# A linear-attention and FFN layer on eight cores: the bf16 copy of x goes from ScalarE to VectorE, the weight ring gets a sixth slot, and the hand-placed early weight loads go

## The chip, the cores and the metric

The kernel runs on all 8 cores of one Trainium2 chip. Each core runs the same program on its own tokens and nothing is exchanged between cores. The metric is the device time of the slowest core, in microseconds (us). PE is TensorE, ACT is ScalarE, DVE is VectorE, POOL is GpSimd and SP is SyncE; PEld is the weight load of TensorE.

## The reference

```python
xn = layernorm(x)                       # x: (4, 4096, 1024) f32, over the last axis, no scale or bias

qkv = xn @ Wqkv + bqkv                  # attention part
q, k, v = split(qkv, 3)
q = q / norm(q);  k = k / norm(k)
kv = sum(k * v, axis=tokens)            # one vector of 1024 for each batch
attn = (q * kv) @ Wout + bout

h = silu(xn @ w1.T * s1) * (xn @ w2.T * s2)      # FFN part, 1024 -> 4096
h = gelu(h @ h1.T * t1)                          # 4096 -> 4096
h = gelu(h @ h2.T * t2)                          # 4096 -> 4096
ffn = h @ w3.T * s3                              # 4096 -> 1024

out = x + attn + ffn
```

## The kernel before

**Tiles.** Two cores share one batch of 4096 tokens. A core writes the output of its own 2048 tokens, but the sum over tokens `kv` needs k and v of all 4096, so it computes those for the other half too. Everything is kept feature-major: features on the 128 partitions, 1024 tokens (`TT`) in the free dimension. The 4096 tokens are four groups g = 0 to 3 of 1024 tokens; 0 and 1 are the core's own. A group of x is 8 chunks (`DC`) of 128 features by 1024 tokens, 512 KB each in f32. The normalised chunks of a group lie in bf16 in one of three regions of the large buffer `Gb` (`REGION`, `xn_sl`).

**Statistics of a group** (`plan_stats`, line 201). For each of the 8 chunks: SP loads the chunk into one of two slots `xs` (`dma_x`, line 181); ACT copies it to bf16 into its region (line 211) and frees the slot; ACT squares the copy into one of two slots `sq` (line 222); PE multiplies a matrix of ones by the copy into PSUM `PA` (the sum) and, two chunks behind, by the square into `PB` (`qmm`, line 237). That is four 128x512 matmuls a chunk. Then DVE and ACT form mean and inverse deviation (lines 250 to 264), and DVE rewrites the 8 chunks in place as normalised values, two operations each (`emit_xn`, lines 273 and 276).

**Weights.** All weights come as units of 128x2048, 1 MB of f32 in HBM, cast to bf16 (512 KB) by a DMA that POOL issues (`dma_w`, line 189) into a ring of five slots `wr`. A load waits until the unit that lay in the slot has been used by PE, and POOL issues strictly in program order.

**Order of the work.** The program is written out by hand, and each engine follows it in order. `Sched.op` adds a wait on the engine's own last operation to every ACT and DVE instruction. First block:

1. statistics of group 0, then loads of the four k units. The first of these loads waits for nothing; the other three have a gate (line 408): they wait for PE's sum over chunks 1, 3 and 5 of group 0;
2. k projection of group 0 (`plan_proj` with `k_evac`), whose results ACT moves out of PSUM and squares; the loads of the four v units, with a gate on the sum over the last chunk of group 0 (line 463); the norm of k (ACT Ln and Exp, lines 319 and 323);
3. statistics of group 1, v projection of group 0, `plan_kv` (DVE: k times v times norm, summed over tokens);
4. k projection of group 1, its norm, statistics of group 2, q projection of group 0, v projection of group 1, `plan_kv` again.

Then all engines meet at the end of the block. The second block begins with the statistics of group 3 and the first FFN layer (w1, w2), goes on with k and v of groups 2 and 3, the layers h1, h2, and the last layer with Wout and w3, and repeats the FFN for the second 1024 tokens.

Two orders matter here. On ACT, the copies of group 1 stand behind the 16 evictions and squares of the k projection and behind Ln and Exp; so do those of group 2. On POOL, a load that waits holds up all loads behind it.

```python
            st["pre_k"] = [dma_w(wqkv[4, :, :])] + [
                dma_w(wqkv[4 + i, :, :], gate=ck0[2 * i - 1][0]) for i in (1, 2, 3)]
```

Of the kernel before, what the change touches and what calls it, by code (L numbers as in the profile page):

```python
# [7 lines left out]
BF16 = mybir.dt.bfloat16  # L8
AF = mybir.ActivationFunctionType
# [4 lines left out]
TT = 1024  # L14
# [5 lines left out]
REGION = {0: 0, 1: 1, 2: 2, 3: 1, 4: 0, 5: 2}  # L20
# [86 lines left out]
def build_program(stop=None):  # L107
    nc = bass.Bass("TRN2", target_bir_lowering=False)

    x_hbm = nc.dram_tensor("x_fm", [D, T], F32, kind="ExternalInput").ap()  # L110
    wqkv = nc.dram_tensor("wqkv_t", [12, 128, 2048], F32, kind="ExternalInput").ap()
# [12 lines left out]
    with ExitStack() as _ctx:  # L124
# [11 lines left out]
        tmp_f = en(nc.sbuf_tensor("tmp_f", [128, TT], F32))  # L136
        xs0 = en(nc.sbuf_tensor("xs0", [128, TT], F32))
        xs1 = en(nc.sbuf_tensor("xs1", [128, TT], F32))
        xb0 = en(nc.sbuf_tensor("xb0", [128, TT], BF16))
        xb1 = en(nc.sbuf_tensor("xb1", [128, TT], BF16))  # L140
        sq0 = en(nc.sbuf_tensor("sq0", [128, TT], BF16))
        sq1 = en(nc.sbuf_tensor("sq1", [128, TT], BF16))
        sil0 = en(nc.sbuf_tensor("sil0", [128, TT], BF16))
# [8 lines left out]
        PB = en(nc.psum_tensor("PB", [128, TT], F32))  # L152
        PC = en(nc.psum_tensor("PC", [128, TT], F32))
        PD = en(nc.psum_tensor("PD", [128, TT], F32))
        semnames = ["s_xa", "s_xb", "s_wa", "s_wb", "s_wc", "s_wd", "s_we",
                    "s_oa", "s_ob", "s_ini", "s_pe", "s_dv", "s_ac", "s_po",
                    "s_ba", "s_bb"]
        sem_h = {n: en(nc.semaphore(n)) for n in semnames}
# [1 line left out]
        dma_sems = [n for n in semnames if n not in ("s_pe", "s_dv", "s_ac")]  # L160
        S = Sched(nc, sem_h, dma_sems)
        xs_ring = Ring([xs0, xs1], ["s_xa", "s_xb"])
        xb_ring = Ring([xb0, xb1], ["s_ba", "s_bb"])
        sq_ring = Ring([sq0, sq1])
        sil_ring = Ring([sil0])
        os_ring = Ring([os0, os1], ["s_oa", "s_ob"])
        w_ring = Ring([wr0, wr1, wr2, wr3, wr4], ["s_wa", "s_wb", "s_wc", "s_wd", "s_we"])
        PS = {"PA": PA, "PB": PB, "PC": PC, "PD": PD}
        psum_free = {k: None for k in PS}
        war = {0: None, 1: None, 2: None}  # L170
# [4 lines left out]
        def xn_sl(g, kc, hh=None):  # L175
            base = REGION[g] * DC * TT + kc * TT
            if hh is None:
                return Gb[:, base: base + TT]
            return Gb[:, base + hh * 512: base + (hh + 1) * 512]
# [9 lines left out]
        def dma_w(unit_ap, gate=None):  # L189
            j, slot, ftok = w_ring.next()  # L190
            tok = S.op("gpsimd", lambda e, o=slot, i=unit_ap: e.dma_start(out=o[:, :], in_=i),  # L191
                       waits=[ftok, gate], inc=w_ring.semn[j])
            return j, slot, tok
# [7 lines left out]
        def plan_stats(g, psS="PA", psQ="PB", defer_xn=False, via_region=True):  # L201
            t0 = T0MAP[g]
            pend = []
            last_q = [None]
            chunk_toks = {}
            for c in range(DC):
                if len(pend) >= 2:
                    pend.pop(0)()
                jx, xslot, tx = dma_x(c, t0)
                if via_region:  # L210
                    tb = S.op("scalar", lambda e, g_=g, c_=c, i=xslot: e.activation(  # L211
                        xn_sl(g_, c_), i[:, :], AF.Identity),
                        waits=[tx, war[REGION[g]]], inc="s_ac")
                    sq_src = xn_sl(g, c)
                else:
                    jb, bslot, fb = xb_ring.next()
                    tb = S.op("vector", lambda e, o=bslot, i=xslot: e.tensor_copy(o[:, :], i[:, :]),
                              waits=[tx, fb], inc="s_dv")
                    sq_src = bslot[:, :]
                xs_ring.set_free(jx, tb)  # L220
                jq, qslot, fq = sq_ring.next()
                tq = S.op("scalar", lambda e, o=qslot, i=sq_src: e.activation(o[:, :], i, AF.Square),
                          waits=[tb, fq], inc="s_ac")
                tok_s = None
                for hh in range(2):
                    rhs = xn_sl(g, c, hh) if via_region else bslot[:, hh * 512:(hh + 1) * 512]
                    tok_s = mm(psS, hh, ones_sb[:, :], rhs,
                               start=(c == 0), stop=(c == DC - 1),
                               waits=[tb, psum_free[psS]],
                               inc="s_pe" if hh == 1 else None)  # L230
                if via_region:
                    chunk_toks[c] = [tok_s, tq]
                    st["chunk_toks_%d" % g] = chunk_toks
                else:
                    xb_ring.set_free(jb, [tok_s, tq])

                def qmm(c_=c, jq_=jq, qslot_=qslot, tq_=tq):
                    tok_c = None
                    for hh in range(2):
                        tok_c = mm(psQ, hh, ones_sb[:, :], qslot_[:, hh * 512:(hh + 1) * 512],  # L240
                                   start=(c_ == 0), stop=(c_ == DC - 1),
                                   waits=[tq_, psum_free[psQ]],
                                   inc="s_pe" if hh == 1 else None)
                    sq_ring.set_free(jq_, tok_c)
                    last_q[0] = tok_c
                pend.append(qmm)
            while pend:
                pend.pop(0)()
            t_stats = last_q[0]
            t1 = S.op("vector", lambda e, p=psS: e.tensor_scalar(  # L250
                tmp_f[:, :], PS[p][:, :], float(1.0 / D), None, ALU.mult),
                waits=[t_stats, st["act_tmp_u"]], inc="s_dv")
            t2 = S.op("scalar", lambda e: e.activation(u_b[:, :], tmp_f[:, :], AF.Square),
                      waits=[t1], inc="s_ac")
            t3 = S.op("vector", lambda e, p=psQ: e.scalar_tensor_tensor(  # L255
                rstd_b[:, :], PS[p][:, :], float(1.0 / D), u_b[:, :], ALU.mult, ALU.subtract),
                waits=[t2], inc="s_dv")
            psum_free[psS] = t1
            psum_free[psQ] = t3
            t4 = S.op("scalar", lambda e: e.activation(rstd_b[:, :], rstd_b[:, :], AF.Ln, bias=f32(EPS)),  # L260
                      waits=[t3], inc="s_ac")
            t5 = S.op("scalar", lambda e: e.activation(rstd_b[:, :], rstd_b[:, :], AF.Exp, scale=f32(-0.5)),
                      waits=[t4], inc="s_ac")
            t6 = S.op("vector", lambda e: e.tensor_mul(u_b[:, :], tmp_f[:, :], rstd_b[:, :]),
                      waits=[t5], inc="s_dv")
            st["act_tmp_u"] = t2
            st["stats_t5t6"] = (t5, t6)
            xn_toks = []
            xn_toks_g[g] = xn_toks

            def emit_xn(c):
                if via_region:
                    ta = S.op("vector", lambda e, g_=g, c_=c: e.tensor_mul(
                        tmp_f[:, :], xn_sl(g_, c_), rstd_b[:, :]),
                        waits=[t5], inc="s_dv")
                    tb2 = S.op("vector", lambda e, g_=g, c_=c: e.tensor_tensor(  # L276
                        xn_sl(g_, c_), tmp_f[:, :], u_b[:, :], ALU.subtract),
                        waits=[ta, t6, chunk_toks[c]], inc="s_dv")
                else:
                    jx, xslot, tx = dma_x(c, t0)  # L280
                    ta = S.op("vector", lambda e, i=xslot: e.tensor_mul(tmp_f[:, :], i[:, :], rstd_b[:, :]),
                              waits=[tx, t5], inc="s_dv")
                    tb2 = S.op("vector", lambda e, g_=g, c_=c: e.tensor_tensor(
                        xn_sl(g_, c_), tmp_f[:, :], u_b[:, :], ALU.subtract),
                        waits=[ta, t6, war[REGION[g]]], inc="s_dv")
                    xs_ring.set_free(jx, ta)
                xn_toks.append(tb2)

            if defer_xn:
                return emit_xn  # L290
            for c in range(DC):
                emit_xn(c)
# [89 lines left out]
        with (  # L382
# [6 lines left out]
            def plan_kv(kbuf, vbuf, t_rk, kev, vev, rbuf):  # L389
# [13 lines left out]
                    st["kv_dve_par0"] = st["kv_done"]  # L403

            plan_stats(0, "PA", "PB")
            ck0 = st["chunk_toks_0"]
            st["pre_k"] = [dma_w(wqkv[4, :, :])] + [
                dma_w(wqkv[4 + i, :, :], gate=ck0[2 * i - 1][0]) for i in (1, 2, 3)]
            xn_toks_g[4] = xn_toks_g[0]
            for t in range(NT1):  # L410
                kbuf = qkvt if t % 2 == 0 else kB2
# [40 lines left out]
                def v_evac(oc, ps, t_mm, _vb=vbuf, _vev=vev):  # L452
# [6 lines left out]

                plan_proj([(wqkv[4 + i, :, :], [2 * i, 2 * i + 1]) for i in range(4)],  # L460
                          t, k_evac, pre=st.get("pre_k"))
                if t == 0:
                    st["pre_v"] = [dma_w(wqkv[8 + i, :, :],
                                         gate=st["chunk_toks_0"][7][0])
                                   for i in range(4)]
                while pend_n:
                    pend_n.pop(0)()
                if t == 0:
# [6 lines left out]
                if t == NT1 - 1:  # L475
                    plan_qproj(4)
                plan_proj([(wqkv[8 + i, :, :], [2 * i, 2 * i + 1]) for i in range(4)],
                          t, v_evac, pre=st.pop("pre_v", None))
                war[t % 3] = S.pe_tok()
                st["pre_k"] = ([dma_w(wqkv[4 + i, :, :], ) for i in range(4)]  # L480
                               if t + 1 < NT1 else None)
# [361 lines left out]
```

How the kernel before makes its waits and increments, by code:

```python
            def body(eng):  # L69
                for _, fn, waits, tok in items:
                    for wt in waits:
                        sname, val = wt[0], wt[1]
                        key = (ename, sname)
                        if self.done.get(key, 0) >= val:
                            continue
                        eng.wait_ge(self.sems[sname], val)
                        self.done[key] = val
                    if fn is not None:
                        inst = fn(eng)
                        if tok is not None:
                            inst.then_inc(self.sems[tok[0]],
                                          16 if tok[0] in self.DMA_SEMS else 1)
```

## Time and profile before

| | us |
|---|---|
| median of two runs | 3010.55 (3009.04 and 3012.05) |
| the profiled execution | 3009.54 |
| its span on the slowest core (core 5), first to last instruction | 3008.0 |
| spans of the eight cores | 2983.2 to 3008.0 |
| PE busy on core 5 | 2859.7 (95%), 13024 matmuls |
| ACT, DVE busy on core 5 | 487.0 (16%), 347.2 (12%) |
| mean granted clock of TensorE, eight cores | 0.973 to 0.982 |

The span is what the trace shows of the profiled execution; 1.5 us of its time lie around it. All rows below are of core 5, and their times count from the start of its span.

### The profile page before, as it was taken

What the parts mean: (1) busy time and instruction counts of PE and PEld (TensorE: products, weight loads), DVE (VectorE), ACT (ScalarE), POOL (GpSimd) and SP (SyncE); (2) the same over time, 40 slices, a digit from 0 to 9 for tenths busy, and PEclk for the clock granted to TensorE, in tenths of its full rate; (3) what the DMA queues carried; (4) which work ended last, traced back from release to release, by engine and by line L of the source; (5) the groups of instructions that cost most, each with busy time, mean ns of one, the idle gap of its engine ahead of it and who ended that gap; (6) DMA issues with size and microseconds to landing.
All of it is one profiled execution on the core that took longest, in us unless ns stands there. A gap on an engine that the chain in (4) does not pass through costs nothing.

```text
span 3008.0 us, 30367 instructions; the slowest of 8 cores (2983.2 to 3008.0 us)
## 1 busy us (share of the span) xinstructions
PE 2859.7 (95%) x13024; PEld 1276.6 (42%) x13024; DVE 347.2 (12%) x397; ACT 487.0 (16%) x484; POOL 219.9 (7%) x420
## 2 busy tenths in 40 slices
PE   3887899999999999999997899999999999999998
PEld 0332344444444444444443344444444444444443
DVE  3244111451000000000002121100000000000011
ACT  3564211541000000000000131110000000000000
POOL 0000000110000000000000000000000000000000
PEclk7888999999999999999998999999999999999999
DMA  4444344874444444444446644444444444444454
GB/s 107 113 90 91 67 75 78 156 129 82 76 76 77 77 78 77 77 75 75 76 78 139 132 70 79 72 79 76 77 77 77 77 78 77 76 75 75 77 113 104
DMA packets 71412, 260.04 MB, mean 86 GB/s; under 512 B 8176, under 2 KB 8304, under 8 KB 71280
## 3 DMA queue, kind: packets, MB, share of 16 engines
q0 software_dynamic: 59904, 218.13, 43.2%
q1 hardware_dynamic: 11376, 39.97, 4.3%
q8 instruction: 105, 1.72, 0.2%
q14 instruction: 27, 0.22, 0.0%
HBM read 466.74 MB, written 9.44 MB: 158 GB/s over the span
## 4 chain that ended last, share of the span: by engine, by line
PE 85%; DMA 3%; DVE 1%; ACT 1%; issue 0%; SPq 0%; DVEq 0%; ACTq 0%
PE PD L198 24%; PE PC L198 24%; PE PA L198 19%; PE PB L198 19%; DMA xs<-x_fm 2%; DMA out_fm<-os 1%; DVE os L761 1%; DVE os L755 0%; ACT os L727 0%; ACT Gb L211 0%; SPq L765 0%; ACT Gb L590 0%; DVE Ab L540 0%; ACT L617 0%; DVE Gb L697 0%
## 5 line engine op out<-in xcount | busy, mean ns | idle before, releaser
L198 PE MATMUL PC<-Gb,wr 128*128 128x512 bf16 x2080 | 476.9, 382 | 22.5 <-DVE Gb L276 22.5
L198 PE MATMUL PD<-Gb,wr 128*128 128x512 bf16 x2080 | 474.0, 380 | 0.0
L198 PE MATMUL PB<-Gb,wr 128*128 128x512 bf16 x1728 | 392.1, 380 | 4.2 <-DVE rstd_b L255 4.2
L198 PE MATMUL PD<-Ab,wr 128*128 128x512 bf16 x1536 | 352.8, 383 | 31.3 <-ACT os L727 31.3
L198 PE MATMUL PA<-Gb,wr 128*128 128x512 bf16 x1536 | 347.2, 379 | 0.0
L198 PE MATMUL PC<-Ab,wr 128*128 128x512 bf16 x1536 | 347.2, 379 | 0.0
L198 PEld LDWEIGHTS PC<-Gb,wr 128*128 128x128 bf16 x2080 | 203.7, 98 | 274.4 <-issue 32.7
L198 PEld LDWEIGHTS PD<-Gb,wr 128*128 128x128 bf16 x2080 | 204.4, 98 | 247.2 <-issue 3.8
L198 PEld LDWEIGHTS PB<-Gb,wr 128*128 128x128 bf16 x1728 | 169.2, 98 | 210.0 <-issue 7.0
L191 POOL DMA_DIRECT2D wr<-h_t x256 | 135.1, 528 | 1616.6 <-PE PB L198 797.2
L198 PEld LDWEIGHTS PD<-Ab,wr 128*128 128x128 bf16 x1536 | 151.3, 99 | 218.1 <-issue 41.7
L198 PE MATMUL PA<-Ab,wr 128*128 128x512 bf16 x1024 | 231.4, 379 | 2.9 <-DVE Ab L540 1.7
L198 PE MATMUL PB<-Ab,wr 128*128 128x512 bf16 x1024 | 231.5, 379 | 0.0
L198 PEld LDWEIGHTS PC<-Ab,wr 128*128 128x128 bf16 x1536 | 150.3, 98 | 181.2
L198 PEld LDWEIGHTS PA<-Gb,wr 128*128 128x128 bf16 x1536 | 150.1, 98 | 181.4
L198 PEld LDWEIGHTS PA<-Ab,wr 128*128 128x128 bf16 x1024 | 99.9, 98 | 124.3 <-issue 3.8
L198 PEld LDWEIGHTS PB<-Ab,wr 128*128 128x128 bf16 x1024 | 100.1, 98 | 120.9
L755 DVE SCALAR_TENSOR_TENSOR os<-PC,cst,os 128x1024 f32<-128x1024 f32 x8 | 10.3, 1284 | 1079.3 <-PE PC L198 1079.3
L697 DVE TENSOR_TENSOR Gb<-tmp_f,u_b 128x1024 bf16<-128x1024 f32 x8 | 9.8, 1225 | 857.9 <-PE PD L198 857.2
L191 POOL DMA_DIRECT2D wr<-w_t x96 | 50.7, 528 | 697.5 <-PE PD L198 565.3
L198 PE MATMUL PA<-Gb,ones_sb 128*128 128x512 bf16 x64 | 31.5, 594 | 68.3 <-ACT Gb L211 68.3
L668 ACT ACTIVATE Ab<-PA,cst 128x1024 bf16<-128x1024 f32 x16 | 17.8, 1114 | 404.9 <-PE PB L198 404.9
(88 smaller groups left out, 1001.5 us busy)
## 6 DMA issues: line engine op xcount, KB each, us to landing
wr<-h_t POOLq DMA_DIRECT2D x256, 512.0 KB, 5.6
wr<-w_t POOLq DMA_DIRECT2D x96, 512.0 KB, 5.2
xs<-x_fm SPq DMA_DIRECT2D x56, 512.0 KB, 5.3
wr<-wqkv_t POOLq DMA_DIRECT2D x56, 512.0 KB, 6.0
out_fm<-os SPq DMA_DIRECT2D x16, 512.0 KB, 3.2
wr<-wout_t POOLq DMA_DIRECT2D x8, 512.0 KB, 7.4
ustats_scratch<-u_b SPq DMA_DIRECT2D x1, 512.0 KB, 3.7
ustats_scratch<-rstd_b SPq DMA_DIRECT2D x1, 512.0 KB, 8.0
```

Of the source, the lines that this page charges most:

```text
L191: tok = S.op("gpsimd", lambda e, o=slot, i=unit_ap: e.dma_start(out=o[:, :], in_=i), waits=[ftok, gate], inc=w_ring.semn[j])
L198: e.matmul(p[:, h * 512:(h + 1) * 512], l, r, start=a, stop=b),
L668: t_g = S.op("scalar", lambda e, o=oc, p=ps: e.activation(dst[:, o * TT:(o + 1) * TT], PS[p][:, :], AF.Gelu, scale=s_cst[:, s_col0 + o:s_c ...
L697: tb2 = S.op("vector", lambda e, c_=c: e.tensor_tensor(xn_sl(5, c_), tmp_f[:, :], u_b[:, :], ALU.subtract), waits=[ta, t_lr, war[REGION[5] ...
L755: t2o = S.op("vector", lambda e, p=ps, o=oslot, c=oc: e.scalar_tensor_tensor(o[:, :], PS[p][:, :], cst2[:, 32 + c:33 + c], o[:, :], ALU.mu ...
L761: t3o = S.op("vector", lambda e, o=oslot, x_=xslot: e.tensor_add(o[:, :], o[:, :], x_[:, :]), waits=[t2o, tx], inc="s_dv")
```

## The change

It does three things. The bf16 copy of each x chunk in `plan_stats` becomes a DVE `tensor_copy` (shown as CAST) in place of an ACT activation; the square stays on ACT. The buffers `xb0` and `xb1`, whose path was never taken, go, and in their place a sixth weight slot `wr5` joins the ring. The lists `pre_k` (first use) and `pre_v`, with their gates, go: the loads are now issued where the projections ask for them, with no wait but that for a free slot.

```diff
-        xb0 = en(nc.sbuf_tensor("xb0", [128, TT], BF16))
-        xb1 = en(nc.sbuf_tensor("xb1", [128, TT], BF16))
+        wr5 = en(nc.sbuf_tensor("wr5", [128, 2048], BF16))
...
-        w_ring = Ring([wr0, wr1, wr2, wr3, wr4], ["s_wa", "s_wb", "s_wc", "s_wd", "s_we"])
+        w_ring = Ring([wr0, wr1, wr2, wr3, wr4, wr5],
+                      ["s_wa", "s_wb", "s_wc", "s_wd", "s_we", "s_wf"])
...
                 if via_region:
-                    tb = S.op("scalar", lambda e, g_=g, c_=c, i=xslot: e.activation(
-                        xn_sl(g_, c_), i[:, :], AF.Identity),
-                        waits=[tx, war[REGION[g]]], inc="s_ac")
+                    tb = S.op("vector", lambda e, g_=g, c_=c, i=xslot: e.tensor_copy(
+                        xn_sl(g_, c_), i[:, :]),
+                        waits=[tx, war[REGION[g]]], inc="s_dv")
...
             plan_stats(0, "PA", "PB")
-            ck0 = st["chunk_toks_0"]
-            st["pre_k"] = [dma_w(wqkv[4, :, :])] + [
-                dma_w(wqkv[4 + i, :, :], gate=ck0[2 * i - 1][0]) for i in (1, 2, 3)]
...
-                if t == 0:
-                    st["pre_v"] = [dma_w(wqkv[8 + i, :, :],
-                                         gate=st["chunk_toks_0"][7][0])
-                                   for i in range(4)]
...
                 plan_proj([(wqkv[8 + i, :, :], [2 * i, 2 * i + 1]) for i in range(4)],
-                          t, v_evac, pre=st.pop("pre_v", None))
+                          t, v_evac)
```

The places where instructions move:

POOL at the start of the program, before: the first load waits only for the constants (`s_ini`), the others for PE (`s_pe`).

```order
5 L191 DMA wr0<-wqkv_t 128x2048 [waits s_ini]
6 L191 DMA wr1<-wqkv_t 128x2048 [waits s_pe]
7 L191 DMA wr2<-wqkv_t 128x2048 [waits s_pe]
8 L191 DMA wr3<-wqkv_t 128x2048 [waits s_pe]
9 L191 DMA wr4<-wqkv_t 128x2048 [waits s_pe]
10 L191 DMA wr0<-wqkv_t 128x2048 [waits s_pe]
```

The same place now:

```order
5 L190 DMA wr0<-wqkv_t 128x2048 [waits s_ini]
6 L190 DMA wr1<-wqkv_t 128x2048
7 L190 DMA wr2<-wqkv_t 128x2048
8 L190 DMA wr3<-wqkv_t 128x2048
9 L190 DMA wr4<-wqkv_t 128x2048
10 L190 DMA wr5<-wqkv_t 128x2048
11 L190 DMA wr0<-wqkv_t 128x2048 [waits s_pe]
```

Six loads now stand one behind the other with no wait between them; the first wait on PE comes with the seventh.

ACT before, from the end of the k projection of group 0 (eviction into `qkvt`, its square), over Ln and Exp (lines 319, 323), into the statistics of group 1:

```order
34 L430 ACTIVATE qkvt<-PD,cst 128x1024
35 L435 ACTIVATE sq<-qkvt 128x1024
36 L319 ACTIVATE rstdn_b<-PA 128x1024
37 L323 ACTIVATE rstdn_b<-rstdn_b 128x1024
38 L211 ACTIVATE Gb<-xs 128x1024
39 L222 ACTIVATE sq<-Gb 128x1024
```

ACT now, the same place and on to the end of the statistics:

```order
19 L420 ACTIVATE qkvt<-PD,cst 128x1024
20 L425 ACTIVATE sq<-qkvt 128x1024
21 L312 ACTIVATE rstdn_b<-PA 128x1024
22 L316 ACTIVATE rstdn_b<-rstdn_b 128x1024
23 L218 ACTIVATE sq<-Gb 128x1024 x8
24 L246 ACTIVATE u_b<-tmp_f 128x1024
```

Of the pair copy and square, eight times over, only the eight squares are left behind Exp.

DVE now, from the last normalised chunk of group 0 on (with its waits; `s_xa` and `s_xb` are the loads into the two `xs` slots, `s_dv` is DVE's own):

```order
27 L266 TENSOR_TENSOR tmp_f<-Gb,rstd_b 128x1024 [waits s_dv]
28 L269 TENSOR_TENSOR Gb<-tmp_f,u_b 128x1024 [waits s_dv]
29 L210 CAST Gb<-xs 128x1024 [waits s_xa,s_dv]
30 L210 CAST Gb<-xs 128x1024 [waits s_xb,s_dv]
31 L210 CAST Gb<-xs 128x1024 [waits s_xa,s_dv]
```

The copies of group 1 wait for their loads and for DVE's own work, and no longer stand behind ACT's evictions, nor do they wait for PE.

## Rows read from the trace of the kernel before

**Rows 1.** Waits of PE: for whom, us in total, times, longest; last row included.

```profile
PE PA L198 <- ACT Gb L211: 68.3, 32, 11.3
PE PD L198 <- ACT os L727: 31.3, 6, 10.7
PE PC L198 <- DVE Gb L276: 22.5, 8, 10.9
...
PE PA L198 <- ACT sq L603: 0.4, 1, 0.4
```

**Rows 2.** Stretch, length, busy of PE, PEld, DVE, ACT, POOL, PEclk, DMA, GB/s.

```profile
0.00:315.00 315.00, 215.48 (x816) 81.54 (x816) 113.71 (x124) 156.89 (x146) 13.54 (x29) 0.80 0.44 99
```

**Rows 3.** Timeline of group 1's statistics: start, us, instruction, [idle before, releaser].

```profile
96.75 1.03 PE L198 MATMUL PA<-sq,ones_sb 128*128 128x512 bf16 x4
...
101.39 1.06 ACT L323 ACTIVATE rstdn_b<-rstdn_b 128x1024 f32<-128x1024 f32 x1
102.54 1.06 ACT L211 ACTIVATE Gb<-xs 128x1024 bf16<-128x1024 f32 x1
...
107.36 1.06 ACT L211 ACTIVATE Gb<-xs 128x1024 bf16<-128x1024 f32 x1 [0.33 <-DMA xs<-x_fm]
...
121.58 1.06 ACT L211 ACTIVATE Gb<-xs 128x1024 bf16<-128x1024 f32 x1 [0.44 <-DMA xs<-x_fm]
...
123.59 1.91 PE L198 MATMUL PB<-sq,ones_sb 128*128 128x512 bf16 x4
125.29 4.76 PE L198 MATMUL PC<-Gb,wr 128*128 128x512 bf16 x16
```

**Rows 4.** Timeline around group 2's statistics: end of DVE's `plan_kv`, Exp, q projection.

```profile
177.82 0.16 DVE L398 TENSOR_TENSOR kv_acc<-kv_acc,kvp 128x1 f32<-128x1 f32 x1
...
188.48 1.06 ACT L323 ACTIVATE rstdn_c<-rstdn_c 128x1024 f32<-128x1024 f32 x1
...
211.93 4.11 PE L198 MATMUL PC<-Gb,wr 128*128 128x512 bf16 x16
```

**Rows 5.** Timeline: DVE's last normalised chunk of group 0.

```profile
65.74 1.23 DVE L276 TENSOR_TENSOR Gb<-tmp_f,u_b 128x1024 bf16<-128x1024 f32 x1
```

**Rows 6.** Loads into `xs` from 185 to 212 us, no weight load beside them.

```profile
DMA to landing us min/median/max: 3.5/4.2/4.3
```

**Rows 7.** Timeline of group 0's statistics: first two weight loads, last copy, its end.

```profile
5.36 0.66 POOL L191 DMA_DIRECT2D wr<-wqkv_t  x1 [4.66 <-DMA ones_sb<-ones_bf]
...
15.02 0.53 POOL L191 DMA_DIRECT2D wr<-wqkv_t  x1 [9.00 <-PE PA L198]
...
33.65 1.06 ACT L211 ACTIVATE Gb<-xs 128x1024 bf16<-128x1024 f32 x1 [1.12 <-DMA xs<-x_fm]
...
37.82 1.23 DVE L250 TENSOR_SCALAR tmp_f<-PA 128x1024 f32<-128x1024 f32 x1 [36.61 <-PE PB L198]
```

**Rows 8.** DMA queues, 0 to 45 us: packets, MB, share of 16 engines.

```profile
q1 hardware_dynamic: 1872, 5.36, 39.2%
q0 software_dynamic: 720, 2.62, 35.4%
```

**Rows 9.** Busy time by stretch, the first 40 us, columns as in rows 2.

```profile
0.00:20.00 20.00, 4.74 (x10) 1.01 (x10) 0.07 (x1) 8.37 (x8) 1.39 (x6) 1.00 0.70 156
20.00:40.00 20.00, 9.46 (x22) 2.34 (x22) 1.23 (x1) 10.62 (x11) 1.58 (x3) 0.80 0.87 222
```

**Rows 10.** Loads into `xs` from 276 to 312 us, with three weight loads beside them.

```profile
DMA to landing us min/median/max: 3.5/4.4/11.5
```

**Rows 11.** Timeline, second block: weight loads, group 3's third copy, first FFN matmuls.

```profile
278.26 1.06 POOL L191 DMA_DIRECT2D wr<-w_t  x2 [24.70 <-POOLq L85]
...
279.60 0.53 POOL L191 DMA_DIRECT2D wr<-w_t  x1 [0.28 <-issue]
...
294.49 1.06 ACT L211 ACTIVATE Gb<-xs 128x1024 bf16<-128x1024 f32 x1 [8.27 <-DMA xs<-x_fm]
...
315.69 5.10 PE L198 MATMUL PB<-Gb,wr 128*128 128x512 bf16 x16 [4.15 <-DVE rstd_b L255]
```

More of the change, by code:

```diff
@@ L154, in build_program @@
         PD = en(nc.psum_tensor("PD", [128, TT], F32))
-        semnames = ["s_xa", "s_xb", "s_wa", "s_wb", "s_wc", "s_wd", "s_we",
+        semnames = ["s_xa", "s_xb", "s_wa", "s_wb", "s_wc", "s_wd", "s_we", "s_wf",
                     "s_oa", "s_ob", "s_ini", "s_pe", "s_dv", "s_ac", "s_po",
@@ L162, in build_program @@
         xs_ring = Ring([xs0, xs1], ["s_xa", "s_xb"])
-        xb_ring = Ring([xb0, xb1], ["s_ba", "s_bb"])
         sq_ring = Ring([sq0, sq1])
@@ L210, in plan_stats @@
                 if via_region:
-                    tb = S.op("scalar", lambda e, g_=g, c_=c, i=xslot: e.activation(
-                        xn_sl(g_, c_), i[:, :], AF.Identity),
-                        waits=[tx, war[REGION[g]]], inc="s_ac")
+                    tb = S.op("vector", lambda e, g_=g, c_=c, i=xslot: e.tensor_copy(
+                        xn_sl(g_, c_), i[:, :]),
+                        waits=[tx, war[REGION[g]]], inc="s_dv")
                     sq_src = xn_sl(g, c)
                 else:
[L216 to L219, printed above, removed]
+                    raise NotImplementedError("xb path removed")
                 xs_ring.set_free(jx, tb)
@@ L230, in plan_stats @@
                                inc="s_pe" if hh == 1 else None)
[L231 to L235, printed above, removed]
+                chunk_toks[c] = [tok_s, tq]
+                st["chunk_toks_%d" % g] = chunk_toks
                 def qmm(c_=c, jq_=jq, qslot_=qslot, tq_=tq):
```

## The prediction

> **What bounds the kernel now.** I read the waits of PE first, because PE is busy for 95% of the span: only what PE waits for, and the clock it runs at, can be won. Its longest item is the 68.3 us, in 32 waits, for ACT's bf16 copy of an x chunk; then 31.3 us for an output slot in the last layer and 22.5 us for DVE's normalised chunks at the start [rows 1]. The list ends at 0.4 us, and nobody in it waits for a weight load. All 32 waits for copies lie in the first 315 us, where PE is busy for 215 us and its mean granted clock is 0.80 [rows 2]. The rest of the program is PE at its pace.
>
> So I went through the timeline of the four statistics phases. For group 1, ACT ends Exp at 101.39 + 1.06 = 102.45, begins the first copy at 102.54, and PE starts the next projection at 125.29: 22.8 us for eight chunks [rows 3]. A chunk costs there (121.58 - 107.36) / 5 = 2.84 us: load, copy and square in turn, through two slots. Group 2 shows the same: Exp ends at 189.54, the projection starts at 211.93, 22.4 us [rows 4].
>
> **Part 1: the copies on DVE, group 1.** Behind Exp, ACT keeps eight squares. Its operations follow one another every 102.54 - 101.39 = 1.15 us [rows 3], so the squares take 9.2 us, and the last one's matmuls about 1 us more: 10.2. PE has four matmuls a chunk: 1.03 us for four at full clock, 1.91 at the low clock [rows 3]. At full clock ACT sets the pace. If PE stayed at the low clock, it would set it: 1.15 + 8 x 1.91 = 16.4. I take 11.5, near the first, because PE then has work all the time and three slow chunks, 3 x (1.91 - 1.03) = 2.6, half hidden, would add 1.3 (an estimate). Gain 22.8 - 11.5 = 11.3, between 6.4 and 12.6.
>
> This needs the copies to be done in time. DVE's last normalised chunk of group 0 ends at 65.74 + 1.23 = 67.0 [rows 5], and at 2.84 a chunk the eight copies of group 1 end by 89.7, 12.7 us before Exp ends. That time of DVE lies beside the k projection. The trace shows no cast on DVE. Its bounds are DVE's smallest operation, 0.16 [rows 4], and its usual 128x1024 operation, 1.23 [rows 5]; ACT's copy took 1.06 [rows 3]. I take 1.23, the nearest in shape. What is queued behind the casts on DVE is the mean of group 1, which waits for PE's last square anyway.
>
> The Trainium skill (VectorE: DVE Perf Modes, the perf-mode tier table) says that a tensor_copy of fp32 in SBUF runs at twice the rate of a two-tensor operation; from its figures I estimate 0.69 us for this cast. No row here shows it. By that price only group 3 changes, by 2 us, and the sum below would be 2993.
>
> **Part 2: group 2.** The casts stand behind `plan_kv` of group 0 on DVE, which ends at 177.98, 11.6 us before Exp [rows 4]. Two chunks lie ready, six follow at 2.84: 177.98 + 2 x 1.23 + 6 x 2.84 = 197.5, 7.9 us after Exp. The eighth square could begin 8.1 us after Exp, so loads and squares arrive together. The pace agrees with the landing of 4.2 us alone [rows 6]: (4.2 + 1.23) / 2 = 2.7. I take 11.9 in place of 22.4: gain 10.5. Bounds: no chunk late, gain 12; PE at the low clock, gain 6.
>
> **Part 3: the weight loads at the start.** Here the change costs. Before, the second load is held until PE releases it at 15.02, and so on; the last copy of group 0 begins at 33.65 [rows 7]. Now six loads go out at once. The queues' shares give the price in time of the 16 engines: x loads 0.392 x 45 / 10 = 1.76 us each (the queue also carried the small constants), weight loads 0.354 x 45 / 5 = 3.19 us each [rows 8]. Until 33.65, eight x loads and four weight loads are 14.1 + 12.8 = 26.9 us in the 28.6 us from about 5 on: 94% busy. With six it is 33.2 us, at 94% 35.3, and the last chunk lands near 40.4: 7 us later. Everything behind it (mean, deviation, the normalised chunks for which PE waits) moves with it, as PE has nothing else to do there. The lower bound is 0: the DMA share over the first 40 us is 0.70 and 0.87 [rows 9], which leaves 8.6 us free, and the two further loads are 6.4. The upper bound: all six first, 5 + 19.1 + 3.5 for the two chunks in front = 27.6, the third chunk at 29.4, five more at 2.84, 43.6: 10 us. I stay with 7, since in the second block a chunk of x issued behind three weight loads took 11.5 us to land, in place of 4.2 [rows 6, 10]: x does not come first.
>
> The Trainium skill (DMA: Bandwidth & Descriptors, Queues, rings and completion order) says that each DMA engine takes turns between its queues packet by packet. With equal packets x would have 1.76 / (1.76 + 3.19) = 0.36 of the time, and a chunk would take some 4.9 us; the 11.5 us of rows 10 say that it was served worse than that. By the rule the last chunk would land near 38.3 and the sum would be 2993.
>
> What the early loads bring is nothing: PE never waited for one. POOL has nothing behind them but later loads.
>
> **Part 4: group 3.** It opens the second block, and its region is free only then, so nothing moves ahead. With six slots four weight loads go out there instead of three (two and one) [rows 11], 3.19 us more in front of chunks 2 to 7: a loss of 0 to 3.2. From the third copy at 294.49 to the first FFN matmul at 315.69 are 21.2 us [rows 11]. With casts beside the squares: two slot rounds of 1.23 + 4.2, the last pair of casts 2.5, a square 1.1, its matmuls 1, and the same 4.2 of mean and deviation give 19.7 to 20, a gain of 1.4; were the casts shorter, up to 3.4. I count 0, between 3 lost and 3.4 gained.
>
> **Part 5: the sixth slot elsewhere.** Each load is still released by the end of a unit, one load per unit; only the unit it brings is one further on. As PE waits for none of them, this is 0. If this cover were missing, a late load would cost PE up to its 3.19 us.
>
> **Sum.** - 11.3 - 10.5 + 7 + 0 = - 14.8. Against the profiled execution's 3009.54: 2994.7, say 2995. The median of the runs is 1.0 above that execution, inside their spread of 3, so I leave it there. Which core ends last is decided in the last layer, by the waits for output slots, which differ between cores; I allow some 3 us for that.
>
> **Rivals.**
> - The early loads cost nothing and the casts are short: gains 12.6 and 12, the start 0, group 3 + 3.4: 28 us, 2981.5. For it: the free DMA share of rows 9. Against: rows 10.
> - The PE clock stays low in the statistics, so PE paces them: 6.4 + 6 - 7 = 5.4 us gained, 3004. For it: the four matmuls at 123.59 took 1.91 [rows 3]. Against: there PE waited between chunks, and now it would not.
> - Slower: the bursts starve x. If a chunk behind six loads takes twice the 11.5 us of rows 10, the third chunk of group 0 lands near 33, five more at 2.84 give 47: 13.4 us late. The fourth load of the second block costs a third of 11.5, 3.8, less 1.4. With the low gains of 12.4: 13.4 + 2.4 - 12.4 = 3.4 us slower, 3013. It decides from the point where group 0's last cast begins after about 46 us. For it: all eight cores send their bursts at the same time. Against: the DMA engines would have to stand idle, and rows 9 show them busy.
>
> **Chances.** Forecast 0.50; cheap start 0.20; low clock 0.20; starved x 0.08; 0.02 for anything else. The range from 2979 to 3011 takes in the first three with the scatter of the cores and part of the fourth. All of them lie within 2% (60 us, about what a measurement of this kernel can tell from no change): faster by over 2% 0.02, within 0.96, slower by over 2% 0.02.
>
> **What would show it.** Right: PE's waits for the copies fall from 68.3 us to under 35, and some return as waits for squares; from the end of the k norm's Exp to the next projection 11 to 12 us twice; the first mean of group 0 (37.82 before) near 45; group 1's casts done before Exp. Wrong: group 0's mean before 40 or after 50; 16 us from Exp to the projections; casts that wait for loads while PE stands; any wait of PE for a weight load.

## The result, and the profile after

The changed kernel took 2999.8 us (median of 12 runs, lowest 2992.08), the kernel before beside it 3014.51 us (11 runs, lowest 3007.84). The ratio, which leaves disturbed runs out, is 0.9942 with a 95% interval of 0.9926 to 0.9959: 17.5 us faster by 3010, between 12 and 22, or 0.6%. The forecast of 2995 against 3009.54 is a ratio of 0.9952, 14.8 us.

The first place to look is the list of PE's waits. The profiled execution of the changed kernel took 3000.44 us; its slowest core is core 3, with a span of 2998.9 (columns as in [rows 1]).

```profile
PE PA L197 <- DVE Gb L210: 63.1, 16, 11.8
PE PD L197 <- ACT os L713: 29.0, 6, 8.1
PE PC L197 <- DVE Gb L269: 22.5, 8, 10.6
...
PE PB L197 <- ACT sq L218: 2.7, 4, 1.3
```

The wait for the copy is now for DVE, in 16 places instead of 32, but its sum has hardly fallen: 63.1 against 68.3 [rows 1]. By stage, on these two cores, it went from 23.4 to 31.7 in the first 45 us, from 20.5 to 3.5 in groups 1 and 2, and from 24.5 to 27.9 at group 3. So the gain cannot be read from the sum, and the phases must be taken one by one. A mark that every run has is the start of the mean of a group (the DVE operation out of `PA` that follows the last square, line 250 before, 243 after). Read from the timelines and averaged over the eight cores:

| start of the mean, us | group 0 | group 1 | group 2 | group 3 | 0 to 1 | 1 to 2 | 2 to 3 |
|---|---|---|---|---|---|---|---|
| before | 39.7 | 126.5 | 212.9 | 312.5 | 86.8 | 86.5 | 99.6 |
| after | 46.7 | 121.6 | 198.3 | 300.0 | 74.8 | 76.7 | 101.7 |

Group 0 is 7.0 us later, the next two steps are 11.9 and 9.8 us shorter, the last is 2.2 us longer. At the last mark 12.5 us are won.

**Start, timeline of core 3.** The answer to [rows 7]:

```profile
5.23 3.31 POOL L190 DMA_DIRECT2D wr<-wqkv_t  x6 [4.53 <-DMA ones_sb<-ones_bf]
...
10.48 0.69 DVE L210 CAST Gb<-xs 128x1024 bf16<-128x1024 f32 x1 [9.28 <-DMA xs<-x_fm]
...
22.97 0.69 DVE L210 CAST Gb<-xs 128x1024 bf16<-128x1024 f32 x1 [9.72 <-DMA xs<-x_fm]
...
42.89 0.69 DVE L210 CAST Gb<-xs 128x1024 bf16<-128x1024 f32 x1 [2.10 <-DMA xs<-x_fm]
...
45.77 1.23 DVE L243 TENSOR_SCALAR tmp_f<-PA 128x1024 f32<-128x1024 f32 x1 [2.18 <-PE PB L197]
```

Six loads are issued in 3.31 us, and DVE then stands 9.72 us before the third chunk. The landing times of the x loads in the first 45 us, against a median of 4.2 alone [rows 6]:

```profile
DMA to landing us min/median/max: 3.6/6.9/14.1
```

What the 16 DMA engines did meanwhile, same core: queues (as in [rows 8]) and the loads issued, from 11.5 to 14.9 us:

```profile
q0 software_dynamic: 141, 0.53, 101.2%
q1 hardware_dynamic: 3, 0.00, 0.0%
...
xs<-x_fm SPq DMA_DIRECT2D x2, 512.0 KB, 12.8
```

Then from 15 to 35 us:

```profile
q0 software_dynamic: 609, 2.21, 69.1%
q1 hardware_dynamic: 476, 1.75, 32.7%
```

The busy time of 15 to 35 and of 35 to 45 us, columns as in [rows 2]:

```profile
15.00:35.00 20.00, 4.00 (x9) 0.88 (x8) 1.58 (x3) 2.11 (x2) 0.00 (x0) 1.00 1.02 198
35.00:45.00 10.00, 6.50 (x17) 1.65 (x18) 2.58 (x4) 4.22 (x4) 0.00 (x0) 1.00 0.71 200
```

While the third and fourth chunk wait, the weight queue (q0) at first has the engines to itself; afterwards x (q1) has about a third of their time. (A packet counts whole where it starts, so a share can come out slightly over 100%.)

**Group 1, same core.** The answer to [rows 3]:

```profile
98.26 0.69 DVE L210 CAST Gb<-xs 128x1024 bf16<-128x1024 f32 x1 [3.60 <-DMA xs<-x_fm]
...
109.20 1.06 ACT L316 ACTIVATE rstdn_b<-rstdn_b 128x1024 f32<-128x1024 f32 x1
...
110.35 2.20 ACT L218 ACTIVATE sq<-Gb 128x1024 bf16<-128x1024 bf16 x2
...
111.55 1.01 PE L197 MATMUL PB<-sq,ones_sb 128*128 128x512 bf16 x2 [1.27 <-ACT sq L218]
...
112.71 1.06 ACT L218 ACTIVATE sq<-Gb 128x1024 bf16<-128x1024 bf16 x1 [0.16 <-PE PB L197]
...
113.21 1.06 PE L197 MATMUL PB<-sq,ones_sb 128*128 128x512 bf16 x2
...
114.42 5.65 ACT L218 ACTIVATE sq<-Gb 128x1024 bf16<-128x1024 bf16 x5 [0.65 <-PE PB L197]
...
115.66 0.59 PE L197 MATMUL PB<-sq,ones_sb 128*128 128x512 bf16 x2
...
120.64 3.62 PE L197 MATMUL PC<-Gb,wr 128*128 128x512 bf16 x16
```

The last cast is over at 98.95, 11 us before Exp ends at 110.26. From there to the projection it takes 10.4 us where it took 22.8. The first two pairs of matmuls for squares still run at the low clock (1.01 and 1.06 us a pair), and ACT waits 0.16 and 0.65 us for them. From the third pair on they run at the full one (0.59 in the row at 115.66, the fourth pair), and ACT's last five squares go through in 5.65 us, 1.13 each: from there ACT sets the pace. The projection's 16 matmuls now begin at full clock, 3.62 us against 4.76.

**Group 2, same core.** The answer to [rows 4]:

```profile
173.38 0.16 DVE L391 TENSOR_TENSOR kv_acc<-kv_acc,kvp 128x1 f32<-128x1 f32 x1
173.65 1.49 DVE L210 CAST Gb<-xs 128x1024 bf16<-128x1024 f32 x2
...
182.69 1.06 ACT L316 ACTIVATE rstdn_c<-rstdn_c 128x1024 f32<-128x1024 f32 x1
...
187.22 0.69 DVE L210 CAST Gb<-xs 128x1024 bf16<-128x1024 f32 x1 [5.44 <-DMA xs<-x_fm]
...
194.28 0.69 DVE L210 CAST Gb<-xs 128x1024 bf16<-128x1024 f32 x1 [1.89 <-DMA xs<-x_fm]
...
197.63 4.79 PE L197 MATMUL PC<-Gb,wr 128*128 128x512 bf16 x16
```

Here the loads are late. DVE waits 5.44 us for the fifth chunk, the eighth is cast 10.5 us after Exp ends, and Exp to projection takes 13.9 us. Two weight loads, issued at 170.98 and 178.75, go out beside these chunks; x lands there in 5.5 us at the median and 6.5 at most, against 4.2 with no weight load beside it [rows 6].

**Group 3, same core.** The answer to [rows 11]:

```profile
264.63 2.12 POOL L190 DMA_DIRECT2D wr<-w_t  x4 [34.80 <-POOLq L85]
...
283.30 0.69 DVE L210 CAST Gb<-xs 128x1024 bf16<-128x1024 f32 x1 [10.60 <-DMA xs<-x_fm]
...
298.14 0.69 DVE L210 CAST Gb<-xs 128x1024 bf16<-128x1024 f32 x1 [2.71 <-DMA xs<-x_fm]
...
305.85 5.26 PE L197 MATMUL PB<-Gb,wr 128*128 128x512 bf16 x16 [4.15 <-DVE rstd_b L248]
```

Four loads go out instead of three. The third cast comes 18.7 us after the first of them is issued; before, the third copy came 16.2 us after. From it to the FFN it is 22.6 us, against 21.2: all casts wait for x.

### The profile page after: what moved, and what is told of

It reads as the page before. It is cut to its first block, busy times and chain, and to the rows that moved or that the text cites. A ratio compares the mean times of both kernels' runs of the same rounds, so it can differ in the third digit from the quotient of the medians.

```text
span 2998.9 us, 30424 instructions; the slowest of 8 cores (2966.1 to 2998.9 us)
## 1 busy us (share of the span) xinstructions
PE 2852.4 (95%) x13024; PEld 1276.3 (43%) x13024; DVE 369.2 (12%) x429; ACT 453.2 (15%) x452; POOL 220.0 (7%) x420
## 4 chain that ended last, share of the span: by engine, by line
PE 85%; DMA 4%; DVE 1%; ACT 1%; issue 0%; SPq 0%; DVEq 0%; ACTq 0%
PE PD L197 24%; PE PC L197 24%; PE PB L197 19%; PE PA L197 19%; DMA xs<-x_fm 2%; DMA out_fm<-os 1%; DVE os L747 1%; DVE os L741 0%; ACT os L713 0%; DVE Gb L210 0%; SPq L751 0%; ACT Gb L576 0%; DVE Ab L526 0%; ACT L603 0%; DVEq L76 0%
## 5 line engine op out<-in xcount | busy, mean ns | idle before, releaser
L197 PEld LDWEIGHTS PA<-Ab,wr 128*128 128x128 bf16 x1024 | 99.9, 98 | 124.3 <-issue 3.8
L197 PE MATMUL PA<-Gb,ones_sb 128*128 128x512 bf16 x64 | 26.7, 517 | 66.1 <-DVE Gb L210 63.1
L654 ACT ACTIVATE Ab<-PC,cst 128x1024 bf16<-128x1024 f32 x16 | 17.8, 1114 | 405.2 <-PE PD L197 405.2
```

The lines of the kernel that those rows point to most:

```text
L197: e.matmul(p[:, h * 512:(h + 1) * 512], l, r, start=a, stop=b),
L654: t_g = S.op("scalar", lambda e, o=oc, p=ps: e.activation(dst[:, o * TT:(o + 1) * TT], PS[p][:, :], AF.Gelu, scale=s_cst[:, s_col0 + o:s_c ...
```

## The experiments

Theory: the terms are separate. The moved copies win some 11 and 10 us in groups 1 and 2, the early loads cost some 7 at the start, the sixth slot costs a little in the second block and wins nothing. Rivals: the start is late because the copies moved; a part of the gain comes from weights that lie there earlier; the early loads pay back later what they cost. The marks below are averages over the eight cores as in the table above; the ratios are to the kernel before, run beside each kernel on the same chip.

**1. The copies alone.** The kernel before, with only this edit:

```diff
-                    tb = S.op("scalar", lambda e, g_=g, c_=c, i=xslot: e.activation(
-                        xn_sl(g_, c_), i[:, :], AF.Identity),
-                        waits=[tx, war[REGION[g]]], inc="s_ac")
+                    tb = S.op("vector", lambda e, g_=g, c_=c, i=xslot: e.tensor_copy(
+                        xn_sl(g_, c_), i[:, :]),
+                        waits=[tx, war[REGION[g]]], inc="s_dv")
```

Expected:

> The kernel before with the copies of x on VectorE and nothing else: five weight slots, the gates on the early weight loads kept. Measure: start of the mean (TENSOR_SCALAR out of PA) of groups 0 to 3, averaged over the eight cores; before 39.7, 126.5, 212.9 and 312.5 us, after the change 46.8, 121.6, 198.3 and 300.0. Theory (the terms are separate, and the start's 7 us come from six weight loads ahead of x): group 0 at 39 to 40; group 0 to 1 74 to 76 us and group 1 to 2 76 to 78, as after the change; group 2 to 3 98 to 101. The mean of group 3 falls to 288 to 294, so 18 to 24 us faster than before, ratio 0.992 to 0.994. Rival (the start is late because the copies moved): group 0 at 45 to 48, the rest as after the change, group 3 near 300. Rival (a part of the 12 and 10 us won in groups 1 and 2 comes from weights that were loaded earlier or from the sixth slot): the steps from group to group stay above 79 us.

Measured: means at 37.2, 112.8, 190.0 and 289.9; steps 75.5, 77.3, 99.9; ratio 0.9903 (0.9871 to 0.9935). The slowest core's timeline, first and last mean:

```profile
35.60 1.23 DVE L250 TENSOR_SCALAR tmp_f<-PA 128x1024 f32<-128x1024 f32 x1 [2.30 <-PE PB L198]
...
287.71 1.22 DVE L250 TENSOR_SCALAR tmp_f<-PA 128x1024 f32<-128x1024 f32 x1 [3.04 <-PE PB L198]
```

Nearly the whole gain of groups 1 and 2 is there without early loads and without the sixth slot (11.2 of 11.9 and 9.2 of 9.8), so the second rival falls. The start is not late but 2.5 us early, below the range that the theory gave: the copies do not hurt it, they help. Group 3 gains nothing. The ratio lies below the expected 0.992 to 0.994, which its interval takes in.

**2. The early loads alone.** The kernel before without `pre_k` and `pre_v`, five slots, copies on ACT:

```diff
-            st["pre_k"] = [dma_w(wqkv[4, :, :])] + [
-                dma_w(wqkv[4 + i, :, :], gate=ck0[2 * i - 1][0]) for i in (1, 2, 3)]
...
-                          t, v_evac, pre=st.pop("pre_v", None))
+                          t, v_evac)
```

Expected:

> The kernel before without the gates and lists of early loads, copies still on ScalarE, five slots: five weight loads go out at once at the start. Theory: group 0's mean at 43 to 47 (before 39.7), as one load fewer than after the change stands ahead of x; the steps from group to group as before (86.8, 86.5, 99.6 us, each within 1.5); so 4 to 7 us slower than before, ratio 1.001 to 1.003. Rival (the loads are harmless and the moved copies make the start late): group 0 at 39 to 40.5, ratio 1.000.

Measured: means at 45.7, 132.5, 219.5 and 320.8; steps 86.8, 87.0, 101.2; ratio 1.0031 (1.0004 to 1.0058). Timeline of its slowest core: five loads, the third copy, the mean.

```profile
5.28 2.78 POOL L191 DMA_DIRECT2D wr<-wqkv_t  x5 [4.58 <-DMA ones_sb<-ones_bf]
...
24.21 1.06 ACT L211 ACTIVATE Gb<-xs 128x1024 bf16<-128x1024 f32 x1 [8.10 <-DMA xs<-x_fm]
...
46.79 1.23 DVE L250 TENSOR_SCALAR tmp_f<-PA 128x1024 f32<-128x1024 f32 x1 [45.59 <-PE PB L198]
```

ACT stands 8.10 us before its third copy, as DVE does after the change, although the copies have not moved. The start is 6.0 us late, and none of it comes back in the next two steps; the step from group 2 to 3 is 1.7 us longer, a little over the 1.5 allowed, though three loads go out there as before. The first rival falls.

**3. The sixth slot alone.** In the place of the unused buffers:

```diff
-        xb0 = en(nc.sbuf_tensor("xb0", [128, TT], BF16))
-        xb1 = en(nc.sbuf_tensor("xb1", [128, TT], BF16))
+        wr5 = en(nc.sbuf_tensor("wr5", [128, 2048], BF16))
```

Expected:

> The kernel before with a sixth weight slot in the place of the unused xb buffers, gates and copies as before. Theory: the sixth slot buys nothing, and one more load stands ahead of x in the second block: means of groups 0 to 2 as before within 1 us, group 3 1 to 3.5 us later (step from group 2 to 3 101 to 103 in place of 99.6), ratio 1.000 to 1.002. Rival (a deeper ring takes loads out of the way of the last layer's stores, or hides some): ratio below 0.998 with a step from group 2 to 3 as before.

Measured: means at 40.6, 128.0, 215.2 and 316.8; steps 87.4, 87.2, 101.6; ratio 1.0009 (0.9987 to 1.0031). The step from group 2 to 3 is 2.0 us longer, as foretold, but run 2 shows 1.7 in this step without a fourth load, so the 2.0 is hardly clear of the scatter; groups 0 to 2 drifted by 0.9 to 2.2 us, a little more than expected. No gain shows anywhere.

**4. All but the early loads.** The changed kernel with the two lists and their gates put back:

```diff
+            st["pre_k"] = [dma_w(wqkv[4, :, :])] + [
+                dma_w(wqkv[4 + i, :, :], gate=ck0[2 * i - 1][0]) for i in (1, 2, 3)]
...
-                          t, v_evac)
+                          t, v_evac, pre=st.pop("pre_v", None))
```

Expected:

> The changed kernel with the gates on the early loads put back: copies on VectorE, six slots. Theory: as the run with the copies alone, but with the fourth load in the second block: group 0 at 39 to 40, steps 74 to 76 and 76 to 78, step from group 2 to 3 1 to 3 us longer than in that run; group 3's mean at 291 to 296, 6 to 9 us ahead of the changed kernel; ratio to the kernel before 0.992 to 0.995. Rival (the ungated loads pay back later what they cost at the start): no gain over the changed kernel, group 3's mean at 299 to 301.

Measured: means at 37.6, 113.2, 191.1 and 292.6; steps 75.6, 77.9, 101.5; ratio 0.9908 (0.9877 to 0.9939). It is 7.4 us ahead of the changed kernel at the last mark, and 9.1 us at the first. So the early loads cost 9.1 us where the casts are on DVE, and 1.7 of it comes back on the way. Run 2 lost 6.0 with five loads; the 3.1 more are about the 3.19 us of one load, the sixth, for which the sixth slot makes room, but this was not tried apart. The third rival falls, but for those 1.7. Group 0 came 1.4 us earlier and the ratio lower than expected, as in run 1. The total time does not tell runs 1 and 4 from the changed kernel, as the intervals overlap: what the early loads cost rests on the marks.

**5. Fewer loads beside x at the start.** Run 1, with the three gates on the last chunk's sum:

```diff
-                dma_w(wqkv[4 + i, :, :], gate=ck0[2 * i - 1][0]) for i in (1, 2, 3)]
+                dma_w(wqkv[4 + i, :, :], gate=ck0[7][0]) for i in (1, 2, 3)]
```

Expected:

> The run with the copies alone, with the gates of the three later k loads moved to PE's sum over the last chunk of group 0: one weight load instead of four stands beside the eight x loads at the start. Theory (each load beside x costs about its 3.2 us of the DMA engines, down to the pace of the two slots, (4.2 + 0.69) / 2 = 2.45 us a chunk): group 0's mean at 29 to 33 us (copies alone 37.2, before 39.7), the steps as in the run with the copies alone (75.5, 77.3, 99.9), as the k units still land before PE asks for them; 4 to 8 us faster than that run, ratio to the kernel before 0.987 to 0.991. Rival (the start is bound by the two slots and the landing, not by the loads): group 0 at 36 to 38. Rival (the loads are then late): PE waits for a weight load, step from group 0 to 1 above 77.

Measured: means at 33.5, 109.0, 187.0 and 287.1; steps 75.5, 78.0, 100.1; ratio 0.9901 (0.9877 to 0.9924). Timeline of the slowest core: the four held loads, the mean.

```profile
31.99 2.11 POOL L191 DMA_DIRECT2D wr<-wqkv_t  x4 [26.27 <-PE PA L198]
33.32 1.23 DVE L250 TENSOR_SCALAR tmp_f<-PA 128x1024 f32<-128x1024 f32 x1 [3.04 <-PE PB L198]
```

The loads leave only when the last chunk of group 0 is summed, and no wait of PE for a weight load is in the list. The start wins 3.7 us more, just short of the least that was expected: with few loads beside x, the two slots would set the pace, which run 7 tries. The total hardly differs from run 1's, where 4 to 8 us were expected; the 2.8 us by which the last mark is ahead are too few for it to show.

**6. No weight loads beside group 3.** Run 5, and in the second block:

```diff
-                        jw1, w1slot, tw1 = dma_w(w1[gc, :, :])
-                        jw2, w2slot, tw2 = dma_w(w2[gc, :, :])
+                        g3 = st["chunk_toks_3"][7][0] if (t == 0 and gc in (1, 2)) else None
+                        jw1, w1slot, tw1 = dma_w(w1[gc, :, :], gate=g3)
+                        jw2, w2slot, tw2 = dma_w(w2[gc, :, :], gate=g3)
```

Expected:

> As the run with late gates, and in the second block the weight loads of w1 and w2 units 1 and 2 wait for PE's sum over the last chunk of group 3, so none stands beside group 3's x loads. Theory: a chunk there then lands in about 4.2 us instead of 11, so the step from group 2 to 3 falls from 99.9 to 90 to 94; nothing of it is given back later, as the first FFN units take 13.8 us from the loads already there; ratio 0.983 to 0.988. Rival (the late loads make PE wait in the first FFN layer): the step falls as said, but the mean span of the cores does not follow it.

Measured: means at 33.5, 108.8, 185.6 and 276.7; steps 75.3, 76.8, 91.1; ratio 0.989 (0.9869 to 0.9911). The landing times of group 3's x loads on its slowest core, against 3.5/4.4/11.5 [rows 10]:

```profile
DMA to landing us min/median/max: 3.6/3.9/5.9
```

Without weight loads beside them no chunk takes 11 us. The last step is 9.0 us shorter than in run 5. The only wait of PE for a weight load on that core is one of 0.9 us. The total moved less than the marks, just outside the expected ratio; the mean span of the eight cores in the profiled executions fell from 2967.4 to 2963.2, 4.2 of the 10.4 us. So the sign of the rival came (the mean span does not follow), but not its cause. The rest went in the last layer: at ACT's first evictions into `os` run 6 is still 10.2 us ahead of run 5, behind the last layer of the first 1024 tokens 4.4, at ACT's last eviction 4.5 (averages over the eight cores). PE's waits for an output slot are 20.2 us there on average, 16.4 in run 5; they differ by more than that from core to core, and whether this is more than scatter was not tried.

**7. A third x slot.** Run 6, with the bytes of the unused buffers given to x:

```diff
+        xs2 = en(nc.sbuf_tensor("xs2", [128, TT], F32))
...
-        xs_ring = Ring([xs0, xs1], ["s_xa", "s_xb"])
+        xs_ring = Ring([xs0, xs1, xs2], ["s_xa", "s_xb", "s_xc"])
```

Expected:

> As the run before it, with a third slot for x chunks in the bytes that the change gave to the sixth weight slot. Theory: where no weights stand beside x, the pace falls from 2.45 us a chunk towards the engines' 1.76: group 0's mean at 25 to 28, step from group 0 to 1 as before (75.5: the copies were in time), step from group 1 to 2 75 to 76 (the last chunks of group 2 no longer late), step from group 2 to 3 86 to 91; ratio 0.979 to 0.986. Rival (HBM, not the slots, sets the pace, as all cores load at once): group 0 and the last step within 1.5 us of the run before it.

Measured: means at 30.5, 105.6, 179.8 and 267.0; steps 75.2, 74.2, 87.2; ratio 0.9885 (0.9844 to 0.9926). First and last mean of the slowest core:

```profile
30.58 1.23 DVE L248 TENSOR_SCALAR tmp_f<-PA 128x1024 f32<-128x1024 f32 x1 [2.18 <-PE PB L196]
...
269.50 1.23 DVE L248 TENSOR_SCALAR tmp_f<-PA 128x1024 f32<-128x1024 f32 x1 [2.17 <-PE PB L196]
```

The two steps in which x was late are 2.6 and 3.9 us shorter, and the start wins 3.0, less than expected; that the first weight load, which still goes out beside the first chunks, holds it is likely, but was not tried apart. At the last mark it is 45.5 us ahead of the kernel before and 33 ahead of the changed one. The interval of the ratio is wide, the ratio is no better than run 6's, and the expected 0.979 to 0.986 was missed. The intervals of runs 5 and 6 lie below the changed kernel's, run 5's by next to nothing, so run 6 beats both kernels; run 7 beats the kernel before, and its interval just touches the changed kernel's.

## Why the prediction was right

The sum was 14.8 us and 17.5 (12 to 22) were measured. Term by term:

- **Group 1: forecast 11.3, measured 11.9, in run 1 alone 11.2.** The mechanism is shown: the casts end before Exp, and eight squares are left behind it. From Exp to the projection it took 10.4 us where 11.5 were forecast. The 1.3 us for the low clock came to 0.8 (the two waits of ACT); the eight squares took 8.9 where I had 9.2, and the last matmuls 0.6 where I had 1.
- **Group 2: forecast 10.5, measured 9.8, in run 1 alone 9.2.** The last cast ended 11.2 us after Exp (194.28 + 0.69 - 183.75) where the forecast had 7.9, because x was 3.3 us later than I took it to be: I used the pace of chunks with no weight load beside them, and two went out beside these. A third slot takes most of that away (run 7: the step falls to 74.2).
- **Start: forecast 7 lost, measured 7.0, and this was partly luck.** It is the difference of two numbers. The early loads cost 9.1 (run 4 against the changed kernel); I had 7, from the share of the DMA engines, and the upper bound was 10. The forecast kept these engines 94% busy to the end; on core 3 they were full from 15 to 35 us, but at 0.71 from 35 to 45. The moved copies give 2.1 to 2.5 back (runs 4 and 1 against the kernel before), and this term was missing. Part of it can be read: from the last copy to the mean it took 4.2 us [rows 7] and takes 2.9 now.
- **Group 3: forecast 0, measured 2.2 lost.** The fourth load costs about 2 (2.0 in run 3, 1.6 in run 4 against run 1, neither far from the scatter of this step). The 1.4 that the faster tail was to bring did not come, since every cast there waits for its load; run 1 shows 0.3 lost.
- **The sixth slot elsewhere: forecast 0.** Run 3 found no gain.
- **What was to be seen.** Group 0's mean near 45: 46.7. Exp to projection 11 to 12 twice: 10.4 and 13.9 on core 3, 10.4 and 13.5 on the average of the eight. No wait for a weight load: none. But the waits for the copy were to fall under 35 us, and they are 63.1. Groups 1 and 2 held only 20.5 of the 68.3 and lost 17 of them; the forecast had forgotten that what the start and group 3 lose goes into the same item, 31.7 and 27.9 of the 63.1.

The marks give 12.5 us at group 3, the whole program 17.5 with an interval that begins at 12.3. The 5 us between them are not the mechanism, and that the total came so near the forecast is partly luck too. On the average of the eight cores in the profiled executions the lead is 12.9 us from the k and v of groups 2 and 3 to the first evictions of the last layer, 11.7 behind that layer, and 14.2 at ACT's last eviction: behind group 3 it moves by more than half a us only in the two stretches of the last layer. PE's wait for an output slot there is 14.8 to 31.3 us on the eight cores before and 7.2 to 29.0 after, it differs more between cores than between kernels, and the slowest core sets the time. That the rest of the 5 us is scatter of this kind is likely, but not shown.

Of the two rules of the Trainium skill that were weighed, the price of the cast (VectorE: DVE Perf Modes, the perf-mode tier table) is confirmed: 0.69 us estimated, 0.69 measured, where the nearest row had led me to 1.23. The packet turns (DMA: Bandwidth & Descriptors, Queues, rings and completion order) gave x 0.36 of the engines' time and 4.9 us for a chunk beside waiting weight loads; the trace nearly agrees, with 32.7% for x from 15 to 35 us. The 14.1 us are a time to landing, in which a load also waits for its first packet (from 11.5 to 14.9 us no x moved) and for the x load in front of it, and the 11.5 us of [rows 10] are such a time too; the prediction was wrong to read them as a worse share. The dearer price was still the better one, 7 against some 5, with 9.1 measured.

The rival of the low clock is refuted by the pairs of matmuls of 1.01 and later 0.59 us; that of the cheap start by run 2; the starved x is half true: a chunk took 14.1 us, not 23.

## What to carry to other kernels

Issue a load early only if something waits for it: before and after the change PE never waited for a weight, and the loads that went out beside the x chunks delayed the work that all else stood behind. When a small operation moves to another engine, look at what stands ahead of it there: the copy became only 0.4 us shorter, but it left a queue of evictions and could be done 11 us before it was needed. And when a forecast comes out right, take its terms apart: one of them was two errors that cancelled.

## What the runs showed of the hardware

A weight load that POOL begins to issue early in a DVE cast takes longer to issue. Timeline of the changed kernel, core 3:

```profile
82.29 0.69 DVE L210 CAST Gb<-xs 128x1024 bf16<-128x1024 f32 x1 [1.98 <-DMA xs<-x_fm]
82.39 0.72 POOL L190 DMA_DIRECT2D wr<-wqkv_t  x1 [73.85 <-PE PD L197]
...
89.73 0.53 POOL L190 DMA_DIRECT2D wr<-wqkv_t  x1 [6.62 <-PE PA L197]
```

The issue that began inside the cast took 0.72 us and ended 0.13 after the cast; the next, with no cast beside it, took 0.53. Cores 4 and 6 show the same once each (0.62 and 0.67, ended 0.12 after the cast). On cores 0, 2 and 5 an issue that began later in a cast, 0.28 to 0.40 us after its start, took 0.53 to 0.54 and ended 0.12 to 0.24 after it. So none of the six ended sooner than 0.12 us after the cast; between 60 and 260 us no other issue on any core took longer than 0.54. The Trainium skill (SBUF — State Buffer, SBUF: two separate sides) says that GpSimd cannot write its descriptors while DVE copies fp32 in SBUF. These six issues agree with it. It cost 0.2 us at most, and PE waited for no weight load.
